# One ring of eight PSUM banks for a cross attention, in place of three pairs and two single banks

## The reference

```python
def _L0_xattn_ref(x, z, Wq, Wkv, Wo):      # 16 heads of width 16
    Q = (x @ Wq.T).reshape(B, xN, NUM_HEADS, HEAD_DIM)
    KV = (z @ Wkv.T).reshape(B, zN, 2, NUM_HEADS, HEAD_DIM)
    K = KV[:, :, 0]
    V = KV[:, :, 1]
    attn = jnp.einsum('bqhd,bkhd->bhqk', Q, K) * SCALE
    attn = jax.nn.softmax(attn, axis=-1)
    O = jnp.einsum('bhqk,bkhd->bqhd', attn, V).reshape(B, xN, DIM)
    return O @ Wo.T
...
x = x + _L0_attn_ref(_layernorm(x), ...)
x = x + _L0_xattn_ref(_layernorm(x), ctx_512, L0_xattn_Wq, L0_xattn_Wkv, L0_xattn_Wo)
x = x + _L0_ffn_ref(_layernorm(x), ...)
# then the second layer: attention without softmax, cross attention, experts
```

## Time and profile before

| | us |
|---|---|
| median of 3 runs (lowest, highest) | 3377.37 (3372.01, 3384.0) |
| profiled execution, its own time | 3402.53 |
| its span, first to last instruction | 3400.7 |
| first and last matmul of `scores` | 612.8, 1128.6 |
| first and last matmul of `turned_scores` | 628.1, 1137.6 |
| PE busy over the span | 3199.8 (94%) |
| DVE, ACT, POOL busy | 1770.2, 1513.7, 869.1 |

### The profile page before, as it was taken

The page is one execution under the profiler, slowest core; times in us unless marked ns, Lnnn a source line. Parts: engine busy times, 40 slices in busy tenths (PEclk is TensorE's granted clock), DMA queues, the critical chain, the costliest instruction groups (busy, mean ns, idle before and its releaser), DMA issues. The chain is left out here.

```text
span 3400.7 us, 77834 instructions
## 1 busy us (share of the span) xinstructions
PE 3199.8 (94%) x26274; PEld 2361.9 (69%) x26275; DVE 1770.2 (52%) x4700; ACT 1513.7 (45%) x4278; POOL 869.1 (26%) x982
## 2 busy tenths in 40 slices
PE   8999999799999898999998989999999999988992
PEld 6777777466666566777776767777777777756882
DVE  4655555466666543222224654666666666653433
ACT  4555555355555311222222346666666666631220
POOL 1000000211111101333332110223223223235874
PEclk9999999899999899999999999999999999989996
DMA  8600000400000332111113000100000000114786
GB/s 269 176 0 0 0 0 0 144 13 11 11 13 11 101 91 79 30 30 32 29 22 92 0 3 8 35 27 22 16 12 13 14 12 13 46 50 122 205 230 149
DMA packets 136648, 181.30 MB, mean 53 GB/s; under 512 B 36397, under 2 KB 108842, under 8 KB 135549
## 3 DMA queue, kind: packets, MB, share of 16 engines
q1 hardware_dynamic: 84272, 133.96, 12.9%
q0 software_dynamic: 45760, 26.67, 4.8%
q10 hardware_dynamic: 6540, 19.66, 1.7%
HBM read 116.11 MB, written 103.61 MB: 65 GB/s over the span
## 5 line engine op out<-in xcount | busy, mean ns | idle before, releaser
L1309 DVE TENSOR_REDUCE e_nmx<-PS 128x1 f32<-128x361 f32 x416 | 221.5, 532 | 360.6 <-PE PS L1156 354.6
L931 POOL DMA_INDIRECT slot_rows<-r_row,r_rows_now x256 | 257.0, 1004 | 345.8 <-DVE e_p L1316 292.6
L1156 PE MATMUL PS<-e_cT,e_qT 128*128 128x361 f32 x832 | 334.2, 484 | 0.7 <-issue 0.6
L1775 DVE TENSOR_REDUCE b_nmx<-PS 100x2 f32<-100x722 f32 x256 | 225.0, 906 | 181.6 <-PE PS L1569 181.6
L2706 PE MATMUL PS<-c_wgu,c_tile_xT 128*128 x912 | 290.8, 462 | 7.1 <-issue 6.3
L1261 ACT ACTIVATE e_pT<-PS 121x384 f32<-121x384 f32 (+1 forms) x416 | 199.4, 480 | 210.1 <-PE PS L1163 206.3
L1163 PEld LDWEIGHTS PS<-ident,e_p 128*121 128x121 f32 x1248 | 199.1, 185 | 97.3 <-issue 1.8
L1266 ACT ACTIVATE e_p<-PS,e_nmx 128x361 f32<-128x361 f32 x416 | 232.9, 560 | 35.2 <-DVE e_nmx L1309 33.8
L2706 PEld LDWEIGHTS PS<-c_wgu,c_tile_xT 128*128 128x128 f32 x912 | 169.8, 191 | 83.9 <-issue 9.1
L1156 PEld LDWEIGHTS PS<-e_cT,e_qT 128*128 128x128 f32 x832 | 146.1, 191 | 115.8 <-issue 109.1
L2972 POOL DMA_INDIRECT sum<-f_y,f_y_token x128 | 199.6, 1560 | 69.4 <-issue 55.8
(11 more groups left out here) (347 smaller groups left out, 6529.8 us busy)
## 6 DMA issues: line engine op xcount, KB each, us to landing
f_w<-in_f_W SPq DMA_DIRECT2D x64, 384.0 KB
slot_rows<-a_empty SPq DMA_DIRECT2D x1, 21504.0 KB, 65.3
f_xg<-slot_rows SPq DMA_DIRECT2D x64, 336.0 KB
c_wgu<-in_c_GU ACTq DMA_DIRECT2D x8, 1408.0 KB, 6.7
sum<-X SPq DMA_DIRECT2D x2, 3200.0 KB, 57.7
f_sums<-sum SPq DMA_DIRECT2D x16, 384.0 KB
b_cT<-in_ctx_T SPq DMA_DIRECT2D x32, 181.5 KB, 2.3
e_cT<-in_ctx_T SPq DMA_DIRECT2D x32, 181.5 KB
```

The lines of the kernel that those rows point to most:

```text
L931: pool.indirect_dma_start(out=self.rows, in_=self.row[:, u, :], in_offset=None, out_offset=bass.IndirectOffsetOnAxis(ap=self.rows_now[:, u ...
L1156: sr.fill_done(pe.matmul(sr.at(f"s{m}", ROWS, CTX), qT[:, at:at + ROWS], cT[:, u, 0:CTX], start=True, stop=True), f"s{m}")
L1309: dve.tensor_reduce(nmx[:, m:m + 1], sr.at(f"s{m}", ROWS, CTX), AX.X, ALU.max, negate=True).then_inc(max_ready, 1)
L1775: sr.move_done(dve.tensor_reduce(nmx[:, g // PAR % 2, 2 * half:2 * half + 2, 16 * (1 - r)], sr.both(f"s{g}{half}", S, CTX), AX.X, ALU.max, ...
```

## The change

`Pairs` goes. Scores, pieces, w, turned scores and o take single banks from one `Ring` of eight, in the order in which PE fills them. Four names are added that nothing fills (z0 to z3, in the odd steps), so that a turn has 96 uses, 12 for each bank; PE marks them filled and moved at once. DVE's maxima are four instructions a step, of 361 columns each, and ACT's exponentials four of 300 columns. `turn_maxima` and `weigh` wait for the last of a group alone, and the wait for the last values (v12) stands in step 2.

```diff
+    UNUSED = {1: ("z0",), 3: ("z1",), 5: ("z2",), 7: ("z3",)}
...
-        sr = Pairs(k, 0, 3).plan([...])
-        mr = Ring(k, 6, 2).plan(names)
+        def quads(a, n, by):
+            return [f"{a}{group(n, by)}{x}" for x in range(TILES_R)]
+
+        def in_step(n):
+            return [*quads("s", n, SCORED), *PIECES[n], *([] if n % PAR else [f"w{group(n, SHIFTED)}"]), *UNUSED.get(n, ()),
+                    *quads("p", n, TURNED), f"o{group(n, WEIGHED)}"]
+        names = [m for n in range(GROUPS) for m in in_step(n)]
+        mr = Ring(k, 0, 8).plan(names)
+        assert len(names) % 8 == 0
...
 def scores(n, i):
-                    for half in range(2):
-                        sr.wait_free(pe, f"s{g}{half}", i)
+                    for a in range(TILES_R):
+                        mr.wait_free(pe, f"s{g}{a}", i)
                     for a in range(TILES_R):
-                        last = pe.matmul(sr.one(f"s{g}{a // 2}", a % 2, S, CTX),
+                        last = pe.matmul(mr.at(f"s{g}{a}", S, CTX),
-                        if a % 2:
-                            sr.fill_done(last, f"s{g}{a // 2}")
+                        mr.fill_done(last, f"s{g}{a}")
...
 def turned_scores(n, i):
-                    for half in range(2):
-                        sr.wait_free(pe, f"p{g}{half}", i)
+                    for a in range(TILES_R):
+                        mr.wait_free(pe, f"p{g}{a}", i)
...
 def exponents(n, i):
-                    for half in range(2):
-                        sr.wait_full(act, f"p{g}{half}", i)
-                        sr.move_done(act.activation(pT[:, g % 2, 2 * half:2 * half + 2, :],
-                                                    sr.both(f"p{g}{half}", KEYS, CH * S), ACT.Exp), f"p{g}{half}")
+                    for a in range(TILES_R):
+                        mr.wait_full(act, f"p{g}{a}", i)
+                        mr.move_done(act.activation(pT[:, g % 2, a, :], mr.at(f"p{g}{a}", KEYS, CH * S), ACT.Exp), f"p{g}{a}")
...
 def maxima(n, half, i):
-                    sr.wait_full(dve, f"s{g}{half}", i)
-                    sr.move_done(dve.tensor_reduce(nmx[:, g // PAR % 2, 2 * half:2 * half + 2, 16 * (1 - r)],
-                                                   sr.both(f"s{g}{half}", S, CTX), AX.X, ALU.max, negate=True),
-                                 f"s{g}{half}")
+                    for a in range(2 * half, 2 * half + 2):
+                        mr.wait_full(dve, f"s{g}{a}", i)
+                        mr.move_done(dve.tensor_reduce(nmx[:, g // PAR % 2, a, 16 * (1 - r):16 * (1 - r) + 1],
+                                                       mr.at(f"s{g}{a}", S, CTX), AX.X, ALU.max, negate=True), f"s{g}{a}")
```

More of the change, by code:

```diff
@@ L198, in pass_over_in @@
             pe.sem_inc(self.moved[self.bank[m]], 1)
[L201 to L228, removed]
 def layer_norm(dve, ln, step, t, i, xs, stored=None):
@@ L1452, in group @@
             return (n + by) % GROUPS
[L1454 to L1461, removed]
+        def quads(a, n, by):
[3 more added lines that the diff above has]
+                    *quads("p", n, TURNED), f"o{group(n, WEIGHED)}"]
+        led = {m for n in range(GROUPS) for a, by in (("s", SCORED), ("p", TURNED)) if n + by >= GROUPS
+               for m in quads(a, n, by)}
+        led |= {f"w{group(n, SHIFTED)}" for n in range(0, GROUPS, PAR) if n + SHIFTED >= GROUPS}
         led |= {f"o{group(n, WEIGHED)}" for n in range(GROUPS) if n + WEIGHED >= GROUPS}
-        mr = Ring(k, 6, 2).plan(names)
-        mr.ends(TURNS, [m for m in names if m in OWN or (m[0] in "wo" and m not in led)])
+        names = [m for n in range(GROUPS) for m in in_step(n)]
+        mr = Ring(k, 0, 8).plan(names)
+        assert len(names) % 8 == 0
+        mr.ends(TURNS, [m for m in names if m in OWN or (m[0] in "swpo" and m not in led)])
         def ahead(n, by, this, nxt):
@@ L1603, in weigh @@
                     mr.wait_free(pe, f"o{g}", i)
[L1604 to L1608 removed]
+                    mr.wait_moved(pe, back(n, 1, i), f"p{g}{TILES_R - 1}")
                     for c in range(CH):
@@ L1661, in turn @@
                         elif not this:
-                            sr.pass_over_in(pe, i, *[f"s{group(n, SCORED)}{half}" for half in range(2)])
+                            mr.pass_over_in(pe, i, *quads("s", n, SCORED))
+                        if this and n == G - WEIGHED:
+                            values_moved(i)
                         for m in PIECES[n]:
@@ L1674, in turn @@
                         elif not this:
-                            sr.pass_over_in(pe, i, *[f"p{group(n, TURNED)}{half}" for half in range(2)])
+                            mr.pass_over_in(pe, i, *quads("p", n, TURNED))
                         if ahead(n, WEIGHED, this, nxt):
@@ L1855, in _ @@
                 turn(TURNS - 1, True, False)
-        sr.done(TURNS)
         mr.done(TURNS)
```

17 lines of the change are left out of this document (8 added, 9 removed).

## The result

The changed kernel takes 3405.45 us (median of 4 runs, 3402.07 to 3413.73) against 3380.68 before (median of 4, 3372.01 to 3385.92). By the medians it is slower by 24.8 us. The ratio, worked out from the runs side by side and so not quite the quotient of the medians, is 1.0079, with a 95% interval from 1.0058 to 1.0100. The forecast was 3394 in a range of 3379 to 3413, from +17 on 3377.4. (Of all executions reported here one, of e11, took 4003 us at a mean granted clock of 0.77, where that kernel's others had 0.97 to 0.98; it is left out of e11's ratio, and its cause isn't known.)

The account below looks back on a forecast made before the run. TensorE sets the pace, busy 57.3 of 60 us, its scores most often waiting for exponentials. Cost 2.74 less gain 1.63 is +1.11 us a turn, +17 over 15 loop turns on 3377.4: 3394, range 3379 to 3413.

Parts of the forecast that it names:

- third maximum: VectorE's third maximum of a step; turned scores would wait for it, signalled 2.34 us after the scores if nothing intervenes.
- step 3: In a turn of eight steps: division delays the third maximum; turned scores 2.97 us after scores against 1.86, +1.11.
- Cost, scores to turned scores: TensorE's turned scores would wait for single maxima, mostly the third, instead of the first pair: 2.74 us a turn.
- Steps 0, 4 and 6: Steps of a turn; turned scores forecast 2.34, 2.34 and 3.39 us after the scores: 0, +0.48 and +0.92.
- Gain, weighing to scores: Scores would wait for one single exponential, not the pair; TensorE goes on at 0.66 us: 1.63 us a turn saved.
- step 5: Step of a turn; addition to X delays the third maximum, weighing 3.01 us after the scores against 2.78: +0.23.
- Nothing for the rest: Pieces' waits, maxima's turn, unused places, exponentials' work, prologue and last turn: 0 us, ends −3 and +3 for the last two.
- The signals are not dear: Rival: extra completion signals in TensorE's matmul groups cost 12 us, 3406; with dearer maxima +35, 3412; chance 0.13.
- The early bank pays: Rival: first single maximum starts 0.51 us after the scores, when its own matmul is done; −15 us, 3362; chance 0.10.
- no net change: Rival: shorter, earlier maxima bring the third to 2.06 us after the scores; +5 us, 3382; chance 0.17.
- The clock stayed at 1.00: Rival claimed TensorE's idling in steps 3 and 6 lowers its clock: some 90 us, 3480; chance 0.02.
- dearer if weighing to scores stays near 0.83: Stated sign of error: if TensorE's weighing to scores stays near 0.83 us, the change is 24 us dearer, 3418.

Follow-up runs that it names:

- e11: e5 with each bank's wait ahead of its own matmul in scores and the first chunk of turned scores: 3362.4 us, 0.9938 of the kernel before.
- e3: Kernel before, with the first of each loop step's two exponentials taking 300 of its 600 columns: 3358.7 us, 0.9930 of the kernel before.
- e1: Changed kernel with all four maxima of a step ahead of the division and the addition on VectorE: 3381.5 us, 1.0004 of the kernel before.
- e6: e5 with the unused place of step 3 moved ahead of the scores: 3369.1 us, 0.9976 of the kernel before.
- e5: e1 with the maxima's turn, its ring place and its VectorE shift ahead of the scores in even steps: 3369.1 us (one run).
- e9: Changed kernel with each bank's wait ahead of its own matmul in scores and the first chunk of turned scores: 3393.6 us, 1.0042 of the kernel before.
- e4: Changed kernel with TensorE's loop of 15 turns written as 5 passes of three turns: 3427.0 us (one run).
- e10: e1 with the waits split as in e9: 3362.9 us, 0.9954 of the kernel before.

## Why the prediction was right

The direction, the mechanism and where it sits are as forecast. e3 shows the gain alone; of the cost, e1 shows the larger part, what stands ahead of the third maximum, and e6 the wait for a third maximum where the second would do (step 3, 2.35 in e5 and 1.91 in e6). The size was 17 and is 25 us, 1.11 against 1.66 a turn; of the 11 us between the forecast 3394 and the measured 3405, 8 are this and 3 the median of the kernel before, 3380.7 instead of 3377.4. The missing 0.55, by terms:

- *Cost, scores to turned scores: 2.74 forecast, 2.99 measured* (0.06, 0.01, 0, 1.12, 0.59, 0.20, 0.99, 0.02 in steps 0 to 7). Step 3 was right to 0.01 by luck: its third maximum began 0.04 later than forecast and its signal took 0.02 less, and the maximum itself 0.01 less. Steps 0, 4 and 6 were each 0.07 to 0.11 short. Two sizes did it. The first single maximum starts 0.88 or 0.89 after the scores in steps 3, 4 and 5, nearly where the pair's did (0.90), not 0.83: a bank filled one matmul sooner is signalled hardly sooner. And the turned scores start 0.14 to 0.15 after the end of the third maximum in steps 0, 4 and 6 (829.98 to 830.13 in step 4), 0.06 in step 3; I took 0.08 for all. With the waits split (e9) it is 0.05 to 0.06 in all four. In the other direction, maxima are 0.44 apart (1.85 for four of 0.52), not 0.45.
- *Gain, weighing to scores: 1.63 forecast, 1.33 measured.* This is the term with the larger miss, and the one where something was left out. PE is ready at 0.65 in six steps as read from the last turn. But at the turn's end it is 0.90, 0.24 more: e4 and e9 show that this is TensorE going round its loop with four waits ahead of its first matmul, hidden before under the wait for exponentials. And in step 5 it is 0.74: the weighing itself had been held by a maximum, and 0.20 of issue follows (801.49); e9 has 0.65 there.
- *Nothing for the rest* held: prologue and last turn, ACT's four exponentials (0.425 each, forecast 0.42; 1.36 for four, forecast 1.35), the pieces' new waits.

The rivals. The signals are not dear to PE: turned scores to weighing is 0.82 before and after, with four completions in the group instead of two (809.33 to 810.16 is 0.83, 826.21 to 827.03 is 0.82), and scores to the next piece 0.80 against 0.79. By the Trainium skill (TensorE: Matmul & The Clock Gate, "The cost: per-tile semaphore tail") each further completion adds some 26 ns; this trace shows none of it in what PE issues next, and leaves room for it only in when a reader may start, as the first maximum's 0.88, where 0.83 was forecast, would have it. That fits, but no run separates it from the matmuls' own order. "The early bank pays" fell with the same 0.88, and so did "no net change", which needed a third maximum signalled at 2.06 in step 4, where the turned scores started at 2.45. The clock stayed at 1.00 with idle times of 1.1 and 1.26 us; e4's idle time of 3.2 us was followed by the half clock. And the point "dearer if weighing to scores stays near 0.83" came true in one step of eight.

## What to carry to other kernels

A ring in program order waits for the use one lap back, so count, for each fill, which reader that is and what stands ahead of it on its own engine; a finer buffer is no gain where it turns "the first half was read" into "the third quarter was read". When a group's buffers come free one after another, put each wait ahead of its own matmul; by the traces that was worth 8 us in the old kernel and 9 to 11 in the ring (by the medians 11, and 12 to 19 where both kernels ran several times). Where a wait is to be removed, look at what it hides (here the loop's jump with the waits behind it) before its whole length is booked as gain. And before a long loop body is unrolled, look at the queue that loads the program: here three turns in one body meant loading code in every pass, and 3.3 us of idle TensorE at its end.

## What the runs showed of the hardware

- Going round TensorE's loop with a body of one turn: 0.90 us between weighing and scores with the waits for four banks ahead of the first matmul (changed kernel), 0.65 to 0.70 with each wait ahead of its own matmul (e9, e10), 0.65 with the four waits and no jump (e4, inside a pass).
- With a body of three turns the scores behind the jump started 3.95 to 4.12 us after the weighing (four times, 3.3 us or more above 0.65), and 56 loads of 16 KB of the program ran from 680 to 1100 us; with a body of one turn there were none. The clock was at half for most of the 4 us after that idle time (0.57 on average), and at full again in the next 4.
- From the end of the third maximum on VectorE to the turned scores that wait for it: 0.06 us in step 3 and 0.14 to 0.15 in steps 0, 4 and 6 with four waits ahead of the group, 0.05 to 0.06 in all four with each wait ahead of its own matmul (e9). What makes step 3 differ from the others was not tested.
- Four VectorE maxima of 361 columns over 100 partitions take 1.85 us in a row, starts 0.44 apart, each 0.52; two over two banks take 1.73. Finer signals cost 0.12 of 1.8 us.
